# Merging two key blocks of a sliding-window attention before the exponentials, by a minimum, instead of behind them, by a sum

## The chip, the cores and the metric

One core of a Trainium2 chip runs the whole program. The metric is the time of one execution on the device, in microseconds (us); lower is better. The number to be predicted is the median after the change; the median before it is 2237.75 us.

## The reference, cut to what matters

Input `x` is 4 batches of 1024 rows of 1024 numbers, in fp32. Each row is normalised (`xn`). Then two branches are computed and joined as `x + s * g`:

- `s` is attention with 16 query heads, 4 key/value heads and a head size of 64. A query row `i` sees key `j` if `i - 511 <= j <= i`, or if `j < 4` (the sinks) and `j <= i`.
- `g` is the silu of a layer norm over `xn + gate * broadcast`: the gate is a sigmoid of a 1024x1024 product for every row, and the broadcast comes from a recurrent FFN on the last row of each batch (four steps, 1024 to 4096 and back).

The part that the change touches is this:

```python
att = jnp.einsum('bkgqd,bkjd->bkgqj', q, k) * scale
att = jnp.where(mask[None, None, None, :, :], att, -jnp.inf)
att = jax.nn.softmax(att, axis=-1)
y = jnp.einsum('bkgqj,bkjd->bkgqd', att, v)
```

## The kernel before, in words

The program has two stages. The first (`attend`) makes the projections, the attention and the FFN; it writes the attention's output `Y` and the split rows `XS` to HBM. The second (`finish`) makes the gate product and the output product for 32 tiles of 128 rows, and joins the branches. In the trace the first stage ends near 1515 us. Operands of the large products are split into a high and a low part (`x_hi`, `x_lo` and so on), and three products are summed.

**Units.** The attention of a batch is 32 units, numbered 0 to 31: 4 groups of 4 heads by 8 query blocks of 128 rows. Unit `s` has group `s // 8` and query block `qb = s % 8`. A unit's keys are the blocks in reach of the window, at most 5 of 128, each padded to 132 columns, with 4 sink columns behind them (`width_of`). With `qb` of 5, 6 or 7 (units 5 to 7, 13 to 15, 21 to 23, 29 to 31 of each batch, 48 in all) the farthest of the 5 blocks is in reach only above the diagonal, and the query's own block only on and below it. The two triangles fill one block of 128 columns. Such units are called merged (`is_merged`, L124).

**A unit's work.** TensorE makes the scores of heads 0 and 1 into `s_ps` (`scores`, L1033), later those of heads 2 and 3. VectorE adds the mask, turns the sign and scales, writes 660 columns to `probs` and takes the minimum of each row as `neg_max` (`mask_scores`, L1334, one custom operation and a short readout of the accumulator). ScalarE takes `exp(-1 * probs + neg_max)` over the same 660 columns and sums each row into `row_sum` (`exponentials`, L808). VectorE takes the reciprocal of two sums (`invert`, L1351), in merged units adds the farthest block's 128 columns onto the own block's (`merge`, L1357), and divides columns 132 to 660 (`divide`, L1363). One triangle of each block is masked, so that the sum holds one number of either. TensorE then transposes the blocks of the four heads into `t_ps` (`turn_probs`, L1071), ScalarE copies them to `pt` (`take_turned`, L798), POOL separates the merged block's two triangles again by two selects (`split_merged`, L700), and TensorE multiplies with `v` (`values`, L1094). POOL packs the 4 sink columns (`pack_sinks`, L712) behind the last division; they are transposed too, and VectorE's product `take_sinks` (L1389) spreads them into `pt_sink`, which the last matmul of `values` needs (L1131).

**The order of the work.** Each engine has one queue, written out by hand in its own `step(b, s)`. In the step of unit `u` the engines also finish unit `u - 1`:

- TensorE (L1167): scores of heads 0, 1; first two transposes of `u - 1` (they wait for all four divisions, `normed`); projections or FFN tiles; in some units the transpose of a row block of the next batch or of a weight (`turn_later`); scores of heads 2, 3 (they wait for both masks, `masked`); other transposes; projections; values of `u - 1`.
- ScalarE (L818): first copies of `u - 1`; exponentials of heads 0, 1; copies of the high parts of a turned block (`turned_high`, L796); copies; exponential 2; copy; exponential 3; others.
- VectorE (L1438): output copy of `u - 2` (`take_y`, L1387); masks of heads 0, 1; the FFN's sums (`add_sums`, L1423; `add_rows`, L1268); the low parts of a turned block (`turned_low`, L1332); masks of heads 2, 3; in units 21 to 28 the statistics of the next batch's rows (L87, L91); the first pair's reciprocal, sums and divisions; the product of the sinks of `u - 1`; the second pair's; in the same units the normalising of the next rows (L106). In units 26 to 31 of the last batch the split of gate weights stands last (L1499).

```python
def divide_pair(b, s, pair):
    invert(b, s, pair)
    for head in range(2 * pair, 2 * pair + 2):
        if is_merged(unit_of(s)[1]):
            merge(b, s, head)
    for head in range(2 * pair, 2 * pair + 2):
        divide(b, s, head)
```

Blocks are turned (`turned_in`) in units 22 to 29 of the first three batches, and weights in units 2, 4, 6, 10, 12, 18 and 20 of the first.

Of the kernel before, what the change touches and what calls it, by code (L numbers as in the profile page):

```python
# [21 lines left out]
ACT = mybir.ActivationFunctionType  # L22
ALU = mybir.AluOpType
AX = mybir.AxisListType

P = 128
# [8 lines left out]
WB = WINDOW // P  # L35
PADDED = P + 4
# [8 lines left out]
GROUP = HEADS // KV  # L45
UNITS = KV * TB
# [62 lines left out]
def unit_of(s):  # L109


    return s // TB, s % TB
# [11 lines left out]
def is_merged(qb):  # L124


    return qb > WB
# [42 lines left out]
def packed_before(u):  # L170

    return (TB - WB - 1) * (u // TB) + max(0, u % TB - WB - 1)
# [12 lines left out]
def attend(nc, shared, y_stored, WT, Y, BC, XS, x, gate_w, Wq, Wk, Wv, in_gamma, in_beta, agg_w, agg_b, pn_gamma, pn_beta, d1_w, d1_b, d2_w, d2_b,  # L185
           bc_w, bc_b):

    with ExitStack() as ctx:
        def sb(name, shape, dt=F32):
            return ctx.enter_context(nc.sbuf_tensor(name, shape, dt))  # L190
# [4 lines left out]
        def sem(name):  # L195
            return ctx.enter_context(nc.semaphore(name))
# [16 lines left out]
        probs = sb("probs", [P, 2 * GROUP, WIDTH])  # L213
# [71 lines left out]
        scores_ready, masked, exp_done = sem("scores_ready"), sem("masked"), sem("exp_done")  # L285
# [3 lines left out]
        merged, pt_split = sem("merged"), sem("pt_split")  # L289
# [137 lines left out]
        def width_of(qb):  # L427

            return blocks_of(qb) * PADDED - (0 if has_sink(qb) else SINK)
# [38 lines left out]
        with nc.Block() as block:  # L468
# [287 lines left out]
            def _(act):  # L756
# [51 lines left out]
                def exponentials(b, s, head):  # L808
                    _, qb = unit_of(s)
                    u = UNITS * b + s  # L810
                    width = width_of(qb)
                    slot = GROUP * (u % 2) + head
                    act.wait_ge(masked, GROUP * u + head + 1)
                    act.activation(probs[:, slot, 0:width], probs[:, slot, 0:width], ACT.Exp,  # L814
                                   bias=neg_max[:, slot:slot + 1], scale=-1.0,
                                   accum_out=row_sum[:, slot:slot + 1]).then_inc(exp_done, 1)

# [426 lines left out]
            def _(dve):  # L1244
# [89 lines left out]
                def mask_scores(b, s, head):  # L1334
# [6 lines left out]
                    if u == 0 and head == 0:  # L1341
# [6 lines left out]
                                             scale=-SCALE, scalar=-NEG, op0=ALU.add, op1=ALU.min,  # L1348
                                             accum_out=neg_max[:, slot:slot + 1]).then_inc(masked, 1)

                def invert(b, s, pair):  # L1351
                    u = UNITS * b + s
                    part = slice(GROUP * (u % 2) + 2 * pair, GROUP * (u % 2) + 2 * pair + 2)
                    dve.wait_ge(exp_done, GROUP * u + 2 * pair + 2)
                    dve.reciprocal(inv_sum[:, part], row_sum[:, part]).then_inc(inv_ready, 1)

                def merge(b, s, head):  # L1357

                    slot = GROUP * (UNITS * b + s) % (2 * GROUP) + head
                    own = probs[:, slot, WB * PADDED:WB * PADDED + P]  # L1360
                    dve.tensor_tensor(own, own, probs[:, slot, 0:P], ALU.add).then_inc(merged, 1)  # L1361

                def divide(b, s, head):  # L1363
                    _, qb = unit_of(s)
                    u = UNITS * b + s
                    slot = GROUP * (u % 2) + head
                    part = slice(PADDED if is_merged(qb) else 0, width_of(qb))
                    if head % 2 == 0:
                        dve.wait_ge(inv_ready, 2 * u + head // 2 + 1)
                    if is_merged(qb):  # L1370
                        dve.wait_ge(merged, GROUP * packed_before(u) + head + 1)
                    dve.tensor_scalar(probs[:, slot, part], probs[:, slot, part], inv_sum[:, slot:slot + 1], None,  # L1372
                                      ALU.mult).then_inc(normed, 1)

                def divide_pair(b, s, pair):
                    invert(b, s, pair)
                    for head in range(2 * pair, 2 * pair + 2):
                        if is_merged(unit_of(s)[1]):
                            merge(b, s, head)
                    for head in range(2 * pair, 2 * pair + 2):  # L1380
                        divide(b, s, head)

# [46 lines left out]
                def think(b):  # L1429
                    n = Q_LNS + LNS * b + TB  # L1430
                    dve.wait_ge(thought_ready, 2 + 2 * b)
                    ln_statistics(dve, ln, n, thought, B, st[0], mv[0])
# [5 lines left out]
                def step(b, s):  # L1438
                    u = UNITS * b + s
# [8 lines left out]
                        take_y(u - 2)  # L1448
                    mask_scores(b, s, 0)
                    mask_scores(b, s, 1)  # L1450
                    if b and s == 0:
                        if b == 1:
                            dve.wait_ge(bias_loaded, 32)
                        add_rows(b, thought, thought)
                        think(b)
# [18 lines left out]
                    if turned_in(b, s):  # L1474
                        for half in range(2):
                            turned_low(u, turned_in(b, s), half)
                    mask_scores(b, s, 2)
                    mask_scores(b, s, 3)
                    if ahead is not None:
                        stats(b + 1, ahead)  # L1480
                    divide_pair(b, s, 0)
                    take_place(1)
                    if u and has_sink((u - 1) % TB):
# [410 lines left out]
```

## Time and profile before

| what | value |
|---|---|
| times of three runs | 2233.90, 2237.75, 2241.33 us |
| median | 2237.75 us |
| the profiled execution: its time | 2241.33 us |
| its span in the trace | 2239.6 us |
| busy: PE, PEld (its weight loads), DVE, ACT, POOL | 2158.8, 1605.7, 1467.3, 840.9, 239.3 us |
| instructions of DVE, of ACT | 3265, 1793 |
| HBM traffic over the span | 163 GB/s |

PE is TensorE, DVE is VectorE, ACT is ScalarE, POOL is GpSimd, SP is the queue that issues most DMAs. Matmuls are pipelined, so that a busy PE can still be slower than its peak. A row of the trace can stand for several instructions in sequence (x2, x8). A bracket at the end of a row gives the idle time of that engine before it, and what ended it; "issue" is time in which it waited for nothing that the profile shows. Times within the trace count from the span's start.

### The profile page before, as it was taken

Reading aid. Unit: us, or ns where it says so; the run is one execution under the profiler, and the core shown is the slowest. Engines: PE = TensorE matmul, PEld = TensorE weight load, DVE = VectorE, ACT = ScalarE, POOL = GpSimd, SP = SyncE. Lnnn points to the kernel's source line nnn. Section 1 sums busy time; section 2 is a strip of 40 time slices with the busy share of each in tenths; the row PEclk is TensorE's granted clock in tenths of the full one; section 3 lists DMA queues with packets and bytes.
Section 4 is the critical chain, followed back from the end, with each engine's and each line's share of the span. In section 5 each row is a group of like instructions: output and inputs, shape, how many; then the busy total and the mean of one; then the engine's idle time right before and its main releaser. Section 6 shows DMA issues by size and latency. Waiting matters only on the chain. (4 is left out here: it accounts for less than half of the span.)

```text
span 2239.6 us, 35984 instructions
## 1 busy us (share of the span) xinstructions
PE 2158.8 (96%) x13433; PEld 1605.7 (72%) x13433; DVE 1467.3 (66%) x3265; ACT 840.9 (38%) x1793; POOL 239.3 (11%) x510
## 2 busy tenths in 40 slices
PE   7999999999999999999999999988999999999998
PEld 6666666766666676666676666657888888888886
DVE  6465677665667657567665566585676676767767
ACT  2254554444554435455343445462111111111111
POOL 2100111010002011011101000010101010010100
PEclk9999999999999999999999999999999999999999
DMA  7486459533447734545853354545333334243331
GB/s 255 137 275 216 129 186 298 167 134 120 152 159 251 245 104 149 179 137 193 283 173 119 122 185 165 201 165 184 141 109 144 122 122 143 101 150 99 144 132 56
DMA packets 174383, 366.57 MB, mean 164 GB/s; under 512 B 13320, under 2 KB 111880, under 8 KB 159904
## 3 DMA queue, kind: packets, MB, share of 16 engines
q1 hardware_dynamic: 168240, 348.30, 46.6%
q0 software_dynamic: 5568, 14.79, 1.9%
q8 instruction: 90, 1.47, 0.3%
q10 hardware_dynamic: 432, 1.57, 0.2%
q14 instruction: 53, 0.43, 0.1%
HBM read 284.79 MB, written 79.72 MB: 163 GB/s over the span
## 5 line engine op out<-in xcount | busy, mean ns | idle before, releaser
L805 ACT ACTIVATE pt<-t_ps 128x512 f32<-128x512 f32 x432 | 237.4, 595 | 475.4 <-PE t_ps L1090 474.9
L1022 PE MATMUL j_ps<-x_hi,w 128*128 128x512 f32 x1232 | 411.4, 404 | 0.0
L814 ACT ACTIVATE probs<-probs,neg_max 128x660 f32<-128x660 f32 (+5 forms) x512 | 356.8, 703 | 45.3 <-DVE neg_max L1344 45.0
L1344 DVE CUSTOM_DVE_ANT_0 probs<-s_ps,mask 128x660 f32<-128x660 f32 (+5 forms) x512 | 322.2, 667 | 68.4 <-PE s_ps L1057 66.6
L1747 PE MATMUL out_ps<-wo,w 128*128 128x512 f32 x1536 | 353.4, 389 | 2.6 <-DVE w L1804 2.6
L1747 PEld LDWEIGHTS out_ps<-wo,w 128*128 128x128 f32 x1536 | 288.3, 188 | 62.7 <-issue 3.0
L1747 PE MATMUL gate_ps<-x_hi,w 128*128 128x512 f32 x1024 | 281.5, 391 | 4.8 <-PEq L468 4.8
L1022 PEld LDWEIGHTS j_ps<-x_hi,w 128*128 128x128 f32 x1232 | 231.0, 190 | 54.4 <-issue 6.6
L1090 PE MATMUL t_ps<-ident,probs 128*128 128x128 f32 x1728 | 240.6, 280 | 24.4 <-DVE x_lo L1332 12.2
L1057 PE MATMUL s_ps<-k_hi,q 64*128 64x330 f32 (+5 forms) x1664 | 251.5, 330 | 8.8 <-DVE q L1316 5.6
L1057 PEld LDWEIGHTS s_ps<-k_hi,q 64*128 64x128 f32 x1664 | 160.0, 185 | 118.8 <-issue 61.6
L1022 PE MATMUL j_ps<-x_lo,w 128*128 128x512 f32 x616 | 244.2, 396 | 0.0
L1125 PE MATMUL o_ps<-pt,v 128*64 128x256 f32 x1920 | 236.5, 387 | 1.6 <-DVE small_rows L1276 1.4
L1090 PEld LDWEIGHTS t_ps<-ident,probs 128*128 128x128 f32 x1728 | 186.0, 141 | 68.0 <-issue 46.4
L1747 PEld LDWEIGHTS gate_ps<-x_hi,w 128*128 128x128 f32 x1024 | 192.9, 189 | 44.9 <-issue 5.0
L1372 DVE TENSOR_SCALAR probs<-probs,inv_sum 128x528 f32<-128x528 f32 (+5 forms) x512 | 207.1, 447 | 5.9 <-DVE probs L1361 0.3
L1125 PEld LDWEIGHTS o_ps<-pt,v 128*64 128x64 f32 x1920 | 127.1, 137 | 93.7 <-issue 42.1
L1734 ACT ACTIVATE b_res<-b_a 128x1024 f32<-128x1024 f32 x32 | 33.9, 1060 | 424.4 <-DVE b_a L1834 424.4
L1747 PE MATMUL gate_ps<-x_lo,w 128*128 128x512 f32 x512 | 158.5, 391 | 0.0
L907 PE MATMUL o_ps<-fw,cols 128*32 128x512 f32 x1088 | 141.9, 605 | 3.3 <-DVE y L1387 1.5
L1057 PE MATMUL s_ps<-k_lo,q 64*128 64x330 f32 (+5 forms) x832 | 135.5, 302 | 0.0
L1022 PEld LDWEIGHTS j_ps<-x_lo,w 128*128 128x128 f32 x616 | 117.1, 190 | 23.5
(182 smaller groups left out, 2317.5 us busy)
## 6 DMA issues: line engine op xcount, KB each, us to landing
fw<-in_L_ffn_d_w_dram SPq DMA_DIRECT2D x128, 1024.0 KB, 5.3
w<-WT SPq DMA_DIRECT2D x36, 1024.0 KB, 5.7
w<-XS SPq DMA_DIRECT2D x64, 512.0 KB, 6.4
XS<-x_hi SPq DMA_DIRECT2D x32, 512.0 KB, 6.9
XS<-x_lo SPq DMA_DIRECT2D x32, 512.0 KB, 8.0
Y<-y SPq DMA_DIRECT2D x256, 64.0 KB, 2.1
b_x<-in_L_attn_x_dram SPq DMA_DIRECT2D x32, 512.0 KB, 4.1
b_y<-Y SPq DMA_DIRECT2D x32, 512.0 KB, 6.5
```

The costliest lines, as they stand in the source:

```text
L805: act.activation(pt[:, m % PT_SLOTS, :, :], bank[:, :].rearrange("p (h q) -> p h q", q=P), ACT.Copy).then_inc(pt_ready, 1)
L814: act.activation(probs[:, slot, 0:width], probs[:, slot, 0:width], ACT.Exp, bias=neg_max[:, slot:slot + 1], scale=-1.0, accum_out=row_sum[ ...
L907: last = pe.matmul(f_ps[COLS * j:COLS * j + COLS, :], cols[:, B * first[j]:B * first[j] + COLS], fw[n % 2][:, bass.ts(j, BANK)], start=sta ...
L1022: last = pe.matmul(bank_of((kind, b, n)), w[:, slot, wp * C + c * P:wp * C + c * P + P], xs[:, c, bass.ts(ch, BANK)], start=i == 0, stop=i ...
L1057: last = pe.matmul(s_ps[head][:, BANK * part:BANK * part + width], qs[h, pair, bass.ts(qb, P)], k[h, g // 2, :, :].rearrange("p t c -> p ( ...
L1090: last = pe.transpose(t_ps[(turns_before(u) + i) % 2][:, bass.ts(head, P)], probs[:, GROUP * (u % 2) + head, PADDED * block:PADDED * block ...
L1125: last = pe.matmul(o_ps[HS * half:HS * half + HS, 0:2 * P], v[:, m * (1 + b % 2), qb - n + 1 + i, half, :], pt[:, (blocks_before(u) + i) % ...
L1344: dve.tensor_tensor_reduce(out=probs[:, slot, 0:width].rearrange("p (a n) -> p a n", a=parts), in0=s_ps[head % 2][:, :].rearrange("p (a n) ...
L1372: dve.tensor_scalar(probs[:, slot, part], probs[:, slot, part], inv_sum[:, slot:slot + 1], None, ALU.mult).then_inc(normed, 1)
L1734: act.activation(res[:, :], a[:, :], ACT.Sigmoid).then_inc(sig2_ready, 1)
L1747: last = pe.matmul(out_[:, bass.ts(half, BANK)], lhs[:, c, :], rhs(c, half), start=(c == 0 and lhs is hi and rhs is w_hi), stop=(c == KB - ...
```

## The change

In merged units the two blocks are merged before the exponential instead of after the reciprocal. At that point `probs` holds the sign-turned scores, in which a masked position is a huge positive number; the smaller of two numbers is the one that isn't masked. VectorE now takes this minimum of 128x128 once for each head, directly behind the masks of heads 0 and 1, and behind each of the masks of heads 2 and 3. Each minimum waits for its own head's mask. ScalarE's exponential waits for the minimum and takes columns 132 to 660, 528 instead of 660. The additions go. Units that aren't merged are unchanged.

```diff
--- before.py
+++ after.py
@@ -810,8 +810,12 @@
                     u = UNITS * b + s
                     width = width_of(qb)
                     slot = GROUP * (u % 2) + head
-                    act.wait_ge(masked, GROUP * u + head + 1)
-                    act.activation(probs[:, slot, 0:width], probs[:, slot, 0:width], ACT.Exp,
+                    part = slice(PADDED if is_merged(qb) else 0, width)
+                    if is_merged(qb):
+                        act.wait_ge(merged, GROUP * packed_before(u) + head + 1)
+                    else:
+                        act.wait_ge(masked, GROUP * u + head + 1)
+                    act.activation(probs[:, slot, part], probs[:, slot, part], ACT.Exp,
                                    bias=neg_max[:, slot:slot + 1], scale=-1.0,
                                    accum_out=row_sum[:, slot:slot + 1]).then_inc(exp_done, 1)
 
@@ -1348,17 +1352,21 @@
                                              scale=-SCALE, scalar=-NEG, op0=ALU.add, op1=ALU.min,
                                              accum_out=neg_max[:, slot:slot + 1]).then_inc(masked, 1)
 
+                def merge(b, s, head):
+
+                    u = UNITS * b + s
+                    if not is_merged(unit_of(s)[1]):
+                        return
+                    slot = GROUP * (u % 2) + head
+                    own = probs[:, slot, WB * PADDED:WB * PADDED + P]
+                    dve.wait_ge(masked, GROUP * u + head + 1)
+                    dve.tensor_tensor(own, own, probs[:, slot, 0:P], ALU.min).then_inc(merged, 1)
+
                 def invert(b, s, pair):
                     u = UNITS * b + s
                     part = slice(GROUP * (u % 2) + 2 * pair, GROUP * (u % 2) + 2 * pair + 2)
                     dve.wait_ge(exp_done, GROUP * u + 2 * pair + 2)
                     dve.reciprocal(inv_sum[:, part], row_sum[:, part]).then_inc(inv_ready, 1)
-
-                def merge(b, s, head):
-
-                    slot = GROUP * (UNITS * b + s) % (2 * GROUP) + head
-                    own = probs[:, slot, WB * PADDED:WB * PADDED + P]
-                    dve.tensor_tensor(own, own, probs[:, slot, 0:P], ALU.add).then_inc(merged, 1)
 
                 def divide(b, s, head):
                     _, qb = unit_of(s)
@@ -1367,16 +1375,11 @@
                     part = slice(PADDED if is_merged(qb) else 0, width_of(qb))
                     if head % 2 == 0:
                         dve.wait_ge(inv_ready, 2 * u + head // 2 + 1)
-                    if is_merged(qb):
-                        dve.wait_ge(merged, GROUP * packed_before(u) + head + 1)
                     dve.tensor_scalar(probs[:, slot, part], probs[:, slot, part], inv_sum[:, slot:slot + 1], None,
                                       ALU.mult).then_inc(normed, 1)
 
                 def divide_pair(b, s, pair):
                     invert(b, s, pair)
-                    for head in range(2 * pair, 2 * pair + 2):
-                        if is_merged(unit_of(s)[1]):
-                            merge(b, s, head)
                     for head in range(2 * pair, 2 * pair + 2):
                         divide(b, s, head)
 
@@ -1448,6 +1451,8 @@
                         take_y(u - 2)
                     mask_scores(b, s, 0)
                     mask_scores(b, s, 1)
+                    merge(b, s, 0)
+                    merge(b, s, 1)
                     if b and s == 0:
                         if b == 1:
                             dve.wait_ge(bias_loaded, 32)
@@ -1475,7 +1480,9 @@
                         for half in range(2):
                             turned_low(u, turned_in(b, s), half)
                     mask_scores(b, s, 2)
+                    merge(b, s, 2)
                     mask_scores(b, s, 3)
+                    merge(b, s, 3)
                     if ahead is not None:
                         stats(b + 1, ahead)
                     divide_pair(b, s, 0)
```

## Rows read from the trace of the kernel before

**Rows 1.** The page, section 1: busy time of each engine.
```profile
PE 2158.8 (96%) x13433; PEld 1605.7 (72%) x13433; DVE 1467.3 (66%) x3265; ACT 840.9 (38%) x1793; POOL 239.3 (11%) x510
```

**Rows 2.** Busy time by stretch of the span: an attention stretch, then one late unit (23).
```profile
450.00:804.00 354.00, 344.25 (x2476) 242.19 (x2476) 228.76 (x649) 171.54 (x405) 41.38 (x90) 1.00 0.54 175
...
330.73:342.47 11.74, 9.45 (x80) 5.88 (x81) 10.51 (x28) 6.68 (x14) 3.54 (x7) 1.00 0.94 303
```

**Rows 3.** Who waited for whom: us in total, times, longest us.
```profile
PE t_ps L1090 <- DVE probs L1372: 5.9, 10, 0.9
...
PE o_ps L1131 <- DVE pt_sink L1396: 4.6, 6, 0.8
...
DVE inv_sum L1355 <- ACT probs L814: 38.7, 47, 2.8
```

**Rows 4.** Groups of instructions by shape: busy us, mean ns, idle before.
```profile
L1361 DVE TENSOR_TENSOR probs<-probs 128x128 f32<-128x128 f32 x192 | 45.4, 278 | 0.0
...
L814 ACT ACTIVATE probs<-probs,neg_max 128x660 f32<-128x660 f32 x192 | 160.9, 845 | 3.2 <-DVE neg_max L1344 3.0
...
L814 ACT ACTIVATE probs<-probs,neg_max 128x524 f32<-128x524 f32 x64 | 46.1, 726 | 3.9 <-DVE neg_max L1344 3.8
```

**Rows 5.** Timeline of an ordinary merged unit: start us, us, engine, operation.
```profile
603.00 0.84 DVE L1344 CUSTOM_DVE_ANT_0 probs<-s_ps,mask 128x660 f32<-128x660 f32 x1
...
603.78 0.85 ACT L814 ACTIVATE probs<-probs,neg_max 128x660 f32<-128x660 f32 x1
...
604.27 0.69 DVE L1423 TENSOR_TENSOR rows<-o_ps,rows 128x512 f32<-128x512 f32 x1 [0.42 <-PE o_ps L907]
...
605.35 0.85 DVE L1344 CUSTOM_DVE_ANT_0 probs<-s_ps,mask 128x660 f32<-128x660 f32 x1 [0.38 <-PE s_ps L1057]
...
606.96 0.47 DVE L1361 TENSOR_TENSOR probs<-probs 128x128 f32<-128x128 f32 x2
...
607.35 0.89 DVE L1372 TENSOR_SCALAR probs<-probs,inv_sum 128x528 f32<-128x528 f32 x2
...
608.27 0.42 DVE L1396 TENSOR_TENSOR pt_sink<-t_ps,own_pair 48x256 fp32r<-48x256 f32 x1
...
611.91 0.18 PEld L1131 LDWEIGHTS o_ps<-pt_sink,v_sink 48*128 48x128 f32 x1 [0.39 <-issue]
```

**Rows 6.** Timeline of a unit that isn't merged.
```profile
500.66 0.16 DVE L1355 RECIPROCAL inv_sum<-row_sum 128x2 f32<-128x2 f32 x1
...
500.85 1.03 DVE L1372 TENSOR_SCALAR probs<-probs,inv_sum 128x656 f32<-128x656 f32 x2
```

**Rows 7.** Timeline of units 22 and 23 of batch 0.
```profile
329.33 0.38 PE L1131 MATMUL o_ps<-pt_sink,v_sink 48*128 48x256 f32 x1 [0.76 <-DVE pt_sink L1396]
...
330.73 0.86 PEld L1090 LDWEIGHTS t_ps<-ident,probs 128*128 128x128 f32 x8 [0.37 <-DVE probs L1372]
...
332.41 0.84 DVE L1344 CUSTOM_DVE_ANT_0 probs<-s_ps,mask 128x660 f32<-128x660 f32 x1
...
332.53 0.85 ACT L814 ACTIVATE probs<-probs,neg_max 128x660 f32<-128x660 f32 x1
...
334.33 1.09 ACT L796 ACTIVATE x_hi<-t_ps 128x512 fp32r<-128x512 f32 x2
...
342.47 1.09 PE L1090 MATMUL t_ps<-ident,probs 128*128 128x128 f32 x8 [0.73 <-DVE probs L1372]
```

**Rows 8.** Timeline of the end of the last batch.
```profile
1430.35 0.18 PEld L1131 LDWEIGHTS o_ps<-pt_sink,v_sink 48*128 48x128 f32 x1 [0.39 <-DVE pt_sink L1396]
...
1503.82 1.40 DVE L1268 TENSOR_TENSOR small_rows<-o_ps,small_rows 4x512 f32<-4x512 f32 x2
...
1510.05 1.09 PE L1090 MATMUL t_ps<-ident,probs 128*128 128x128 f32 x8 [0.83 <-DVE probs L1372]
```

**Rows 9.** Timeline of POOL: a select, and a copy beside VectorE's L1499.
```profile
603.48 0.64 POOL L706 TENSOR_SCALAR_AFFINE_SELECT pt<-pt 128x512 f32<-128x512 f32 x1 [2.43 <-ACT pt L805]
...
1499.73 2.27 POOL L717 CAST sink_cols<-probs 128x32 fp32r<-128x32 f32 x1 [6.99 <-DVE probs L1372]
```

## The prediction

> **What bounds the kernel now.** I read the page first. TensorE has work in 2158.8 of 2239.6 us, VectorE in 1467.3, ScalarE in 840.9 [rows 1]. By stretches, the attention stage keeps TensorE at 344 of 354 us, its clock granted in full, with VectorE at 229 us [rows 2]. The change touches VectorE and ScalarE only, and only in units whose query block is 5, 6 or 7: 3 of 8 per key group, 12 per batch, 48 in all. So the question is where TensorE waits for one of them. The waits answer it [rows 3]: TensorE stood still for the divided probabilities 10 times, 5.9 us in all, and for the sinks' product 6 times, 4.6 us. VectorE waited for exponentials 47 times, 38.7 us, but that is a wait of an engine that has slack. Whatever becomes of it is gained only where TensorE waits behind it.
>
> The profiled execution took 2241.33 us, 1.7 more than its span and 3.6 above the median of 2237.75. I work out a difference in its trace and add it to the median. About 0.3% (6.7 us) is what a measurement of this kernel can tell from no change.
>
> **The parts and their prices.** (1) *Shorter exponentials.* 192 exponentials go from 660 to 528 columns. One of 660 takes 0.845 us, one of 524 takes 0.726 [rows 4], so 0.12 us goes from each: 23 us of ScalarE, which is no bound.
>
> (2) *Merges out of the divisions.* 192 additions of 128x128 take 0.278 us each [rows 4]. In a pair they overlap: two take 0.47, and the divisions begin 0.08 before their end, so 0.39 per pair [rows 5]. Without them the first division waits for the reciprocal. The unmerged units show that wait: a reciprocal of 0.16 at 500.66, the division at 500.85, 0.03 after its end instead of 0.08 before it [rows 6]. So 0.39 - 0.11 = 0.28 us goes from in front of each pair's divisions.
>
> (3) *Minima instead.* No row has a 128x128 minimum of two tiles. The nearest is the sum of the same tiles, 0.278, the same operands under another operator, so I take that. As bounds I keep half and double of it, 0.14 and 0.56. The minima of heads 0 and 1 stand behind both masks and add 0.39. Those of heads 2 and 3 each wait for the mask operation just in front: they start 0.03 after its end, last 0.28, and the next starts 0.08 before their end. Against the old overlap of 0.08 that is 0.31 each, 0.62 for two.
>
> Of that wait the Trainium skill says otherwise (VectorE: DVE Perf Modes, The DRAIN you can't avoid): a semaphore between two Vector instructions costs nothing, since the pipe empties anyway. By it the two minima would add 0.40 and each pair would lose 0.39, and the sum below would be some 1.8 us lower (0.44 in each of four units). The rows differ: 0.11 us lies between start with and without a wait [rows 5, 6].
>
> (4) *Ordinary merged units.* At 603.00 the mask of head 1 starts and ends at 603.84. VectorE then idles 0.42 until 604.27, does the FFN sum and idles 0.38 until 605.35 [rows 5]. The 0.39 of minima fit into the first gap. If that cover were gone they would cost 0.39 in each of 48 units, 19 us. The first exponential starts near 604.1, when the first minimum is there, instead of 603.78 and the two give 0.24 back, so ScalarE is free for its next copies at most 0.1 later. Then the masks of heads 2 and 3 with minima are 0.62 later, the first divisions 0.62 - 0.28 = 0.34, the sinks' product 0.34, the last divisions 0.62 - 0.56 = 0.06. The sinks' product is done at 608.69 and TensorE comes to it at 611.91 [rows 5], so 0.34 is hidden. Price: nothing.
>
> (5) *The units where VectorE is the bound.* In units 22 and 23 of the first three batches (numbered from 0), VectorE also takes the next batch's rows (statistics, low parts, normalising): 10.5 busy of 11.7 us [rows 2]. In unit 22 TensorE stands 0.76 us for the sinks' product [rows 7]: it comes 0.34 later. It next waits for probabilities (0.37 between weight loads), which swallows a part; how much is left doesn't matter, since the longer wait of unit 23 comes right behind. In unit 23 the mask of head 0 ends at 332.49 and the exponential starts at 332.53. Head 1's mask ends at 333.25. Now the first exponential needs the first minimum: 333.17 + 0.28, with 0.06 from before and 0.04 for the signal, 333.55. That is 1.02 later. Two exponentials give back 0.24. ScalarE's copy of the turned rows, which follows them without a gap at 334.33, is 0.78 later, and with it the low parts, both masks and all that VectorE has behind them [rows 7]. The last divisions add 0.06. TensorE waited 0.73 us for them at 342.47; it goes on 0.84 later, which holds what was left of unit 22's delay. Price 3 x 0.84 = **2.5 us**. Unit 6 of batch 0 and units 29 turn a block too, but without VectorE's other load: I take nothing, and at worst another 0.84 each.
>
> (6) *The end of batch 3.* In unit 31 VectorE goes from head 1's mask straight to the last FFN rows (1503.82), so nothing hides the 0.39, and TensorE waits for the divisions at 1510.05 [rows 8]: 0.39 + 0.06 = **0.45 us** later. Where the last divisions wait for ScalarE they come up to 0.24 + 0.28 = 0.52 earlier; TensorE isn't waiting there, and I count nothing.
>
> No DMA is added, moved or renamed. The queues of SP and POOL keep their order. POOL's wait for the last division moves by 0.06.
>
> Sum: 2.5 + 0.45 = +3.0 us, so 2237.75 + 3.0 = **2240.7 us**, no change that can be told.
>
> **Rivals.** *A, slower: the sinks' product ends the values everywhere.* Place: the sinks' product stands between the two pairs of divisions and moves 0.34 later in all 48 merged units. If TensorE stands there each time, 48 x 0.34 = 16.3 us, 2254. It decides from the point where the product has less than 0.34 us to spare. For it: TensorE already waited there in 6 units. Against: at 608.69 against 611.91 it has 3.2 us, and in unit 22 of batch 3 the gap before the values' last weight load (1430.35) is 0.39, as without a wait at 611.91, though the profile names the product there [rows 5, 8]: near the point, not past it. Chance 0.08.
>
> *B, faster: the chain through the exponentials carries the end.* The last divisions would come 0.24 + 0.28 = 0.52 us earlier where they wait for ScalarE. The 10 stops for probabilities, 5.9 us in all, would go: 2231.9. If TensorE stood there in all the 47 places of VectorE's wait it would be 24 us, 2213, but rows 3 have only 10. Against it: at the largest of them (unit 23, unit 31) VectorE is busy, not waiting. Chance 0.08.
>
> *C: the minima of heads 0 and 1 now run beside POOL's selects.* Before, the sums never did. The select at 603.48 lasts 0.64 [rows 9] and a second follows it; the minima stand at 603.76 to 604.24. A POOL copy of 32 columns took 2.27 us beside VectorE operations with two SBUF operands [rows 9], so these two do share something, and there POOL was the one held. If POOL is held here too, its selects end up to 0.47 later, and TensorE needs them only in the second half of the values, which end near 612. If VectorE is held, which no row shows, the minima wait up to 0.36, or 1.06 behind both selects. That is hidden in ordinary units but delays unit 22's first exponential by up to 0.8 and unit 23's by 0.2: 3 x 1.0 = 3 us more, 2243.7. The Trainium skill (Advanced Engine Details and Errata, VectorE Performance Modes) has it that GpSimd and two-port Vector instructions share the second SBUF port and block each other. It names no loser. Chance of C: 0.11.
>
> **Chances.** Forecast 0.68, C 0.11, both within 0.3%: 0.79. A 0.08, and 0.05 for a later wait that I don't see: slower 0.13. B 0.08: faster. Range: the forecast gives -1 to +6 us (a minimum at 0.56 adds 0.56 or 0.84 us in each of the seven units of parts 5 and 6), the runs before spread over 2233.9 to 2241.3, and C adds 3. I give 2233 to 2248; A and the lower half of B lie outside.
>
> **What would show it.** Right: exponentials of 528 columns at 0.73 us; 192 minima at 0.28; TensorE's wait for unit 23's probabilities from 0.73 to about 1.5 us, three times; its wait for the sinks' product from 0.76 to about 1.1 in unit 22 and more in unit 23; ordinary merged units as long as before. Wrong: minima above 0.35 or POOL's selects above 0.64 (C); stops for the sinks' product in far more than 6 units (A); fewer stops for probabilities than 10 (B); a first exponential of unit 23 no later than before, which would take away my 2.5 us.

## The result: 0.2% slower, about 4.9 us

Over 22 runs each, the changed kernel took 2244.85 us (2241.31 to 2248.51), the kernel before 2241.01 (2232.76 to 2245.71). The ratio is 1.0022 with a 95% interval of 1.0014 to 1.0030: 4.9 us more, between 3.1 and 6.7. That is real and below the 0.3% that the prediction set as its bound. The time of 2240.7 was forecast from 2237.75, so +3.0, which lies just below this interval. Of the 4.2 us by which 2244.85 exceeds 2240.7, 3.3 are the kernel before itself: it took 2241.01 here, not 2237.75.

**The profile after.** The profiled execution took 2243.06 us, its span 2241.3. The page's busy times, which answer to [rows 1]:

```profile
PE 2155.3 (96%) x13433; PEld 1602.0 (71%) x13433; DVE 1490.3 (66%) x3265; ACT 824.8 (37%) x1793; POOL 243.2 (11%) x510
```

The groups by shape, which answer to [rows 4]: busy us, mean ns, idle before.

```profile
L1363 DVE TENSOR_TENSOR probs<-probs 128x128 f32<-128x128 f32 x192 | 57.9, 321 | 3.3
...
L818 ACT ACTIVATE probs<-probs,neg_max 128x528 f32<-128x528 f32 x192 | 140.4, 733 | 23.3 <-DVE probs L1363 23.2
...
L706 POOL TENSOR_SCALAR_AFFINE_SELECT pt<-pt 128x512 f32<-128x512 f32 x48 | 30.7, 639 | 117.3 <-ACT pt L805 117.3
...
L709 POOL TENSOR_SCALAR_AFFINE_SELECT pt<-pt 128x512 f32<-128x512 f32 x48 | 34.2, 713 | 3.3
```

ScalarE has its gift: 845 ns became 733, 192 times. VectorE didn't get the sum back for the same price: 278 ns became 321, and it is busy 23 us longer. The second of POOL's two selects, at 713 ns, was 637 before. The waits (us in total, times, longest) answer to [rows 3]. TensorE's for the sinks' product and for the low parts of turned rows grew (from 4.6 and 12.2); its wait for probabilities didn't:

```profile
PE t_ps L1094 <- DVE x_lo L1336: 14.8, 18, 1.3
...
PE o_ps L1135 <- DVE pt_sink L1399: 7.4, 7, 1.1
PE t_ps L1094 <- DVE probs L1378: 5.5, 11, 0.9
```

**Where the time went.** TensorE's order of work is the same in both kernels, so I measured from one output copy (`y<-o_ps`) to the next and compared the 127 steps. "The step of unit u" is the one in which VectorE masks and divides unit u.

| step of unit | before | after |
|---|---|---|
| 22, batches 0 to 2 | 13.30 | 13.45 |
| 23, batches 0 to 2 | 11.74 | 12.66 |
| 6, then 7, of batch 0 | 12.51, 13.34 | 12.83, 13.28 |
| 15, batch 3 | 10.33 | 10.64 |
| 22, batch 3 | 9.75 | 9.87 |
| 29, batch 3 | 10.97 | 10.46 |
| 31, batch 3 | 9.19 | 9.72 |

These sum to 3 x 1.07 + 0.26 + 0.31 + 0.12 - 0.51 + 0.53 = **+3.9 us**. The other merged units take the same time within 0.06 us, apart from two steps that differ without the change too. Unit 23 of batch 3 went from 9.43 to 9.12, but it is also 9.07 or 9.08 in three kernels with the old order there (experiments 2, 8 and 9). Unit 29 of batch 1 went from 16.00 to 16.37, but unit 28 in front of it from 14.29 to 14.00, and the kernel before, profiled again, has 14.35 and 16.06. In the last batch the steps of units 11, 28 and 30 are no measure: from profile to profile, whatever the kernel, they lie between 12.0 and 13.6, 9.2 and 10.6, 10.6 and 11.5. The timeline of units 22 and 23 of batch 0 shows how it comes about (against [rows 7]):

```profile
315.82 0.65 POOL L706 TENSOR_SCALAR_AFFINE_SELECT pt<-pt 128x512 f32<-128x512 f32 x1 [3.89 <-ACT pt L805]
...
316.10 0.71 DVE L1363 TENSOR_TENSOR probs<-probs 128x128 f32<-128x128 f32 x2
316.54 0.77 POOL L709 TENSOR_SCALAR_AFFINE_SELECT pt<-pt 128x512 f32<-128x512 f32 x1
...
328.49 0.64 POOL L709 TENSOR_SCALAR_AFFINE_SELECT pt<-pt 128x512 f32<-128x512 f32 x1
...
328.77 0.69 DVE L1363 TENSOR_TENSOR probs<-probs 128x128 f32<-128x128 f32 x2
...
329.30 0.74 ACT L818 ACTIVATE probs<-probs,neg_max 128x528 f32<-128x528 f32 x1 [1.11 <-DVE probs L1363]
...
330.75 1.06 ACT L796 ACTIVATE x_hi<-t_ps 128x512 fp32r<-128x512 f32 x2
...
332.57 0.83 DVE L1348 CUSTOM_DVE_ANT_0 probs<-s_ps,mask 128x660 f32<-128x660 f32 x1
...
332.80 1.06 PE L1094 MATMUL t_ps<-ident,probs 128*128 128x128 f32 x8 [1.31 <-DVE x_lo L1336]
...
333.45 0.29 DVE L1363 TENSOR_TENSOR probs<-probs 128x128 f32<-128x128 f32 x1
333.65 0.84 DVE L1348 CUSTOM_DVE_ANT_0 probs<-s_ps,mask 128x660 f32<-128x660 f32 x1
...
337.85 0.38 PE L1135 MATMUL o_ps<-pt_sink,v_sink 48*128 48x256 f32 x1 [1.14 <-DVE pt_sink L1399]
...
338.98 1.09 PE L1094 MATMUL t_ps<-ident,probs 128*128 128x128 f32 x8 [0.46 <-DVE probs L1378]
```

Read it from 328.77. The two minima take 0.69 where two sums took 0.47 [rows 5], since POOL's second select lies beside them. ScalarE has stood idle 1.11 us for the first one. Behind the two exponentials comes the copy of turned rows, and TensorE waits 1.31 us for the low parts made from it (0.55 before), then 1.14 for the sinks' product (0.76 before). It finds the last divisions a little nearer: 0.46 instead of 0.73. The two other waits in the kernel before:

```profile
336.40 1.07 PE L1090 MATMUL t_ps<-ident,probs 128*128 128x128 f32 x8 [0.55 <-DVE x_lo L1332]
...
341.07 0.38 PE L1131 MATMUL o_ps<-pt_sink,v_sink 48*128 48x256 f32 x1 [0.76 <-DVE pt_sink L1396]
```

The sum 0.76 + 0.38 - 0.27 is 0.87 of the step's 0.92. One minimum between two masks costs 1.08 from start to start instead of 0.76: 0.32.

**The minima and the selects.** The single instructions, as number and shortest, median and longest ns: the minima and the second select after, then the second select before.

```profile
L1363 DVE TENSOR_TENSOR probs<-probs x192: 276/291/510, 134.3 to 1507.5; 128x128 f32<-128x128 f32 x192
L709 POOL TENSOR_SCALAR_AFFINE_SELECT pt<-pt x48: 636/770/776, 145.9 to 1512.5; 128x512 f32<-128x512 f32 x48
...
L709 POOL TENSOR_SCALAR_AFFINE_SELECT pt<-pt x48: 636/637/640, 150.7 to 1512.2; 128x512 f32<-128x512 f32 x48
```

In 30 of the 48 units the pair of minima meets a select, and each time the one that started later is the one that lasts longer. A select that is already under way keeps its 0.64 us, and the first minimum takes 0.49 to 0.51; the second takes 0.28. In 27 units the second select starts beside the minima, and takes 0.77. In unit 22 above, the first minimum (316.10, 0.51) ends 0.14 behind the select that started at 315.82.

**Units 15 and 29 of batch 3.** In unit 15 the minima stand in front of an FFN result (`h_pre`) that TensorE waits for. Before, after, and with the doubled minima of experiment 4:

```profile
1345.78 0.42 PE L1057 MATMUL s_ps<-k_hi,q 64*128 64x330 f32 x2 [0.32 <-DVE h_pre L1406]
...
1346.82 0.42 PE L1061 MATMUL s_ps<-k_hi,q 64*128 64x330 f32 x2 [0.64 <-DVE h_pre L1409]
...
1348.48 0.42 PE L1061 MATMUL s_ps<-k_hi,q 64*128 64x330 f32 x2 [1.48 <-DVE h_pre L1415]
```

In unit 29 VectorE waits less for the last exponentials, and the output copy behind its last divisions, for which TensorE waits at the start of unit 30, comes sooner. Two rows before, two after:

```profile
1487.72 0.17 DVE L1355 RECIPROCAL inv_sum<-row_sum 128x2 f32<-128x2 f32 x1 [0.94 <-ACT probs L814]
...
1491.75 2.01 PE L907 MATMUL o_ps<-fw,cols 128*32 128x512 f32 x16 [1.52 <-DVE y L1387]
...
1487.77 0.17 DVE L1369 RECIPROCAL inv_sum<-row_sum 128x2 f32<-128x2 f32 x1 [0.34 <-ACT probs L818]
...
1491.54 1.92 PE L911 MATMUL o_ps<-fw,cols 128*32 128x512 f32 x16 [1.05 <-DVE y L1390]
```

Whether this gain of 0.5 lasts to the end isn't shown, since the step of unit 30 differs by more from profile to profile.

### The profile page after: what moved, and what is told of

Its sections match the earlier page's. It is cut to its first block and busy times, and to the rows that moved or that the text cites. A ratio compares the mean times of both kernels' runs of the same rounds, so it can differ in the third digit from the quotient of the medians.

```text
span 2241.3 us, 35888 instructions
## 1 busy us (share of the span) xinstructions
PE 2155.3 (96%) x13433; PEld 1602.0 (71%) x13433; DVE 1490.3 (66%) x3265; ACT 824.8 (37%) x1793; POOL 243.2 (11%) x510
## 5 line engine op out<-in xcount | busy, mean ns | idle before, releaser
L818 ACT ACTIVATE probs<-probs,neg_max 128x528 f32<-128x528 f32 (+5 forms) x512 | 336.3, 661 | 65.1 <-DVE neg_max L1348 41.7
```

The costliest lines, as they stand in the source:

```text
L818: act.activation(probs[:, slot, part], probs[:, slot, part], ACT.Exp, bias=neg_max[:, slot:slot + 1], scale=-1.0, accum_out=row_sum[:, slo ...
```

## Experiments

All are built from one of the two kernels. Each experiment is compared with runs of the kernel before taken beside it; experiments 5 to 8 are one run each, beside one run of the kernel before, on another chip than the other experiments. The steps below come from their profiles.

**1 and 2. Old order in the seven turned units; new order there alone.** The seven are units 22 and 23 of batches 0 to 2 and unit 6 of batch 0. The first keeps the change elsewhere:

```diff
+def ahead_of(u):
+    b, s = divmod(u, UNITS)
+    return is_merged(s % TB) and (not ((b < B - 1 and s in (22, 23)) or (b == 0 and s == 6)))
...
-                    if not is_merged(unit_of(s)[1]):
+                    if not ahead_of(u):
```

> The changed kernel, but units 22 and 23 of batches 0 to 2 and unit 6 of batch 0 keep the sum behind the exponentials. Theory T (the cost lies where a turned block's copy stands behind the late first exponential: 0.32 us in unit 6, 1.08 us per batch in units 22 and 23, 3.5 us in all): the steps of these units are again as long as before (11.74 us for unit 23), and the time is about 3.5 us below the changed kernel's, at 1.0000 to 1.0007 of the kernel before. Rival R (the cost is spread over all 48 merged units, whose minima run beside POOL's selects and last longer): only 7 of 48 parts go, the ratio stays near 1.0019.

The second is the same with the `not` ahead of the bracket left out.

> The mirror: the kernel before, with the minimum ahead in those seven units alone. T: plus 3.5 us, ratio to the kernel before 1.0015, unit 23's step 12.7 us instead of 11.74, all other merged steps as before. R: plus 0.7 us at most, ratio 1.0003.

Measured: the first 2241.34, ratio 1.0015 (0.9997 to 1.0032), the second 2244.67, ratio 1.0030 (1.0016 to 1.0044). The steps moved as a switch does: 11.74, 13.30 and 12.52 with the old order in those units, 12.66, 13.45 and 12.81 with the new. So these seven units carry 3.5 of the 3.9 us by steps. The times alone don't decide between theory and rival: the first interval holds what both expected (up to 1.0007, and 1.0019), and the second is 6.4 us above the kernel before where 3.5 were expected. The ratio of the first lies 0.0015 above 1 with little in its steps; the section on the clock takes that up.

**3. A minimum behind each mask for all four heads.**

```diff
-                    mask_scores(b, s, 1)
                     merge(b, s, 0)
+                    mask_scores(b, s, 1)
```

> The changed kernel with the order mask 0, minimum 0, mask 1, minimum 1. The first exponential then starts 0.35 us after its old place instead of 1.0, but head 1's mask ends 0.31 later, and TensorE's second scores wait for it. T: unit 23's step falls from 12.66 to about 12.2, units 22 and 23 give back 1 to 1.5 us in all; in ordinary units TensorE comes to that mask 0.29 after its end, so up to 0.05 in each is lost, 2 us: ratio to the kernel before 1.001 to 1.003. R (the VectorE time of the minima is what costs): each minimum behind its mask adds a wait of 0.11, so 0.2 in each of 48 units, 10 us more than the changed kernel, ratio 1.006.

Measured: 2247.9, ratio 1.0045 (1.0028 to 1.0063). Unit 23 gained (12.33 instead of 12.66), since the first exponential starts earlier, but most ordinary merged units lost 0.07 to 0.12 (up to 0.05 was expected), a loss that the changed kernel doesn't have. The ratio lies above the theory's 1.003 and below the rival's 1.006, and its interval reaches both. Units 15 and 31 of batch 3 lost 0.5 more than in the changed kernel (11.13 and 10.24). The gap behind head 1's mask covers a pair of minima there; in front of that mask nothing does.

**4. Twice the minima for heads 0 and 1.** Two more minima of 128x128, on constants, follow in each of the 48 units.

```diff
+                        for n in range(2):
+                            part = mask4[:, 2 * P * n:2 * P * n + P]
+                            dve.tensor_tensor(part, part, part, ALU.min)
```

> The changed kernel with two more 128x128 minima (of a constant tile with itself, which changes nothing) behind those of heads 0 and 1 in all 48 merged units, about 0.4 us of VectorE each. T: they lie in VectorE's idle time, 0.3 us before the FFN sum and 0.4 before head 2's mask in ordinary units, and 1.25 before the low parts in unit 23, so only what exceeds it shows: plus 0 to 4 us on the changed kernel. R: 0.4 in each of 48 units, plus 19 us, ratio to the kernel before about 1.011.

Measured: 2248.63, ratio 1.0050 (1.0030 to 1.0070). Ordinary merged units kept their length even with this load. A theory that the loss is spread over all 48 has to fall: it is in the units where VectorE is late already. Of the 3.8 us above the changed kernel's time, 2.4 are the step of unit 15 of batch 3 (13.04 instead of 10.64), where TensorE's wait for the FFN result grew to 1.48 us.

**5. POOL's selects wait for the minima.**

```diff
+                    if is_merged((u + 1) % TB):
+                        pool.wait_ge(merged, GROUP * packed_before(u + 1) + 2)
```

> The changed kernel, with POOL's selects waiting for the minima of heads 0 and 1 where the next unit is merged too, so that they no longer run beside them. If the selects hold up VectorE: minima of units 22, 23 and their like go from 0.69 to 0.71 us per pair back to 0.47, the mean of 192 from 0.32 to about 0.28, the first exponential of units 22 and 23 starts about 0.2 earlier, and the two steps give back 0.2 to 0.4 us per batch of the 1.08. Rival (the minimum is a slower operation than the sum): the pair stays at 0.7.

Measured, one run: 2242.57 beside 2238.43. The groups by shape of this kernel:

```profile
L1365 DVE TENSOR_TENSOR probs<-probs 128x128 f32<-128x128 f32 x192 | 51.5, 289 | 3.3
...
L711 POOL TENSOR_SCALAR_AFFINE_SELECT pt<-pt 128x512 f32<-128x512 f32 x48 | 30.6, 638 | 3.3
```

Its timeline ahead of unit 23's exponentials:

```profile
327.19 0.49 DVE L1365 TENSOR_TENSOR probs<-probs 128x128 f32<-128x128 f32 x2
...
327.84 0.65 POOL L708 TENSOR_SCALAR_AFFINE_SELECT pt<-pt 128x512 f32<-128x512 f32 x1 [2.06 <-DVE probs L1365]
```

Kept apart, both have their own duration again: 0.49 instead of 0.69, 638 ns instead of 713. Unit 23's step fell to 12.45 (-0.21), unit 22's to 13.41 (-0.04), unit 6's to 12.60 (-0.22), that of unit 15 of batch 3 to 10.44 (-0.20). This is what the contention costs.

**6. Exponentials at their old width.** The exponentials take all 660 columns again, so that the farthest block counts twice in the row sums.

```diff
-                    part = slice(PADDED if is_merged(qb) else 0, width)
+                    part = slice(0, width)
```

> The changed kernel with exponentials over all 660 columns (the sum of a row then counts the farthest block twice over, so that the output is another). T: the 0.12 us per exponential matter only where TensorE waits behind ScalarE: unit 23's step 12.66 to about 12.9, unit 6's 12.83 to 13.07, three batches: plus 1 us, and the gains of batch 3 in steps 29 and 30 (0.5 each) go half away. Rival (shorter exponentials gained nothing): no step moves.

Measured, one run: 2240.93 beside 2238.43; the steps of units 23, 22 and 6 grew to 12.89, 13.67 and 13.05, 0.22 or 0.23 more each: two exponentials of 0.12. Unit 29 of batch 3 lost half of its gain (10.71 instead of 10.46). The shorter exponentials do pay, but only where ScalarE is waited for. The run's total is lower than the changed kernel's although these steps are longer: its mean clock is 0.995, and unit 11 of batch 3 is 0.8 shorter in it. A single run doesn't tell 2 us.

**7. The minima of heads 2 and 3 in a pair.** Both follow head 3's mask, so that neither minimum waits for the mask right in front of it: head 2's mask is done, and head 2's minimum stands between head 3's mask and its minimum.

```diff
-                    merge(b, s, 2)
                     mask_scores(b, s, 3)
+                    merge(b, s, 2)
                     merge(b, s, 3)
```

> The changed kernel with the minima of heads 2 and 3 both behind mask 3, so that no minimum waits for the mask right in front except the last. My price of the wait (0.11 us each): steps of units 22 and 23 are 0.1 to 0.25 shorter together per batch. By the rule that such a wait is free: no step moves.

Measured, one run: 2247.3 beside 2238.43, with steps of 13.20 and 12.43 in units 22 and 23 (-0.25 and -0.23). The pair takes 0.49 and overlaps the work behind it, where single ones cost 0.32 each, so the wait just behind a mask is not free: 0.12 for each of the two. The time itself says nothing here, at a mean clock of 0.990, the lowest of the single runs. Unit 29 lost 0.31 of its gain, probably since head 2's exponential starts later.

**8. The kernel before with a load in unit 23.** One minimum of 128x640 on constants in front of head 2's mask.

```diff
+                    if b < B - 1 and s == 23:
+                        dve.tensor_tensor(mask4[:, 0:5 * P], mask4[:, 0:5 * P], mask4[:, 0:5 * P], ALU.min)
```

> The kernel before, with one 128x640 minimum of a constant tile with itself (0.8 us of VectorE, changes nothing) before head 2's mask in unit 23 of batches 0 to 2, so that TensorE waits longer there as in the changed kernel, with no merge moved. Theory K (TensorE's longer wait in unit 23 is what brings the 3.4 us at granted clock 0.5 right behind it, seen behind 1 of 3 such units in the kernel before and behind 2 or 3 of 3 with the new order): unit 23's step 12.5 us and the slow stretch behind 2 or 3 of 3. Rival (it comes by chance or by the new order itself): behind 0 or 1 of 3.

The load and TensorE's wait in this kernel's timeline:

```profile
333.08 0.81 DVE L1478 TENSOR_TENSOR mask<-mask 128x640 f32<-128x640 f32 x1
...
338.71 0.39 PE L1131 MATMUL o_ps<-pt_sink,v_sink 48*128 48x256 f32 x1 [1.49 <-DVE pt_sink L1396]
```

Measured, one run: 2243.91 beside 2238.43. Some 0.73 us more on VectorE's row (the next mask starts that much later) made TensorE wait 0.73 longer (1.49 for 0.76) and the step 0.74 longer (12.48 for 11.74). Unit 23 has no slack on VectorE in front of head 2's mask: what goes in comes out in the step, one for one. The sign of theory K came too: all three places behind unit 23 show a lowered clock.

**9. The sum behind the exponentials, made by POOL.** If unit 23 has no slack, what leaves VectorE should come back as well. From the kernel before, with the old sum, in units 22 and 23 of batches 0 to 2 and unit 31 of batch 3:

```diff
+                def merge_pair(u, pair):
+                    if not on_pool(u):
+                        return
+                    for head in range(2 * pair, 2 * pair + 2):
+                        slot = GROUP * (u % 2) + head
+                        own = probs[:, slot, WB * PADDED:WB * PADDED + P]
+                        pool.wait_ge(exp_done, GROUP * u + head + 1)
+                        pool.tensor_tensor(own, own, probs[:, slot, 0:P], ALU.add).then_inc(merged, 1)
...
-                        if is_merged(unit_of(s)[1]):
+                        if is_merged(unit_of(s)[1]) and not on_pool(UNITS * b + s):
                             merge(b, s, head)
```

> The kernel before with the sum behind the exponentials kept, but made by POOL instead of VectorE in the seven units that VectorE bounds: 22 and 23 of batches 0 to 2 and 31 of the last batch (28 sums of 128x128). Theory (in these units VectorE's own row is the bound, so what leaves it is gained, and the end of the values moves with the sum, which is not the bound there): 0.28 us per pair is saved where the pair stood between VectorE's mask and its next work, so the steps behind units 22 and 23 become together about 0.6 to 1.1 us shorter in each of three batches and unit 31 about 0.5, 2.5 to 4 us in all: ratio to before about 0.9985. Rival (the values' end, or POOL itself, becomes the bound): POOL's sum of two sources lasts longer than VectorE's 278 ns and stands behind its selects, the last divide and the sinks' product go on waiting for the exponentials, and nothing is gained: ratio 1.000, or a step up to 0.5 us longer in each.

POOL's group of this kernel:

```profile
L725 POOL TENSOR_TENSOR probs<-probs 128x128 f32<-128x128 f32 x28 | 12.5, 454 | 6.2 <-ACT probs L833 5.9
```

Its timeline in unit 23 of batch 0:

```profile
332.18 0.86 POOL L725 TENSOR_TENSOR probs<-probs 128x128 f32<-128x128 f32 x2
332.21 0.42 DVE L1415 TENSOR_TENSOR pt_sink<-t_ps,own_pair 48x256 fp32r<-48x256 f32 x1
...
332.69 0.38 PE L1150 MATMUL o_ps<-pt_sink,v_sink 48*128 48x256 f32 x1 [0.49 <-DVE pt_sink L1415]
332.87 0.96 DVE L1391 TENSOR_SCALAR probs<-probs,inv_sum 128x528 f32<-128x528 f32 x2
```

Measured: **2231.1 us (8 runs), ratio 0.9955 (0.9940 to 0.9971)**, faster than both kernels. POOL needs 454 ns for what VectorE does in 278, but it has the time. The wait for the sinks' product is 0.49 instead of 0.76, and the steps are 12.83 and 11.25 in units 22 and 23 and 8.82 in unit 31, so 3 x 0.96 + 0.37 = 3.2 us less, as expected. The ratio is worth 10 us, where 0.9985 was expected. The rest isn't in these steps.

**10. The change only where it might gain**, in units 21 to 23, 29 and 30 of batch 3 (`return is_merged(s % TB) and b == B - 1 and s in (21, 22, 23, 29, 30)`).

> The change only in five merged units of the last batch (21, 22, 23, 29, 30), old order everywhere else. Theory (the shorter exponentials gain only where the profile of after showed a shorter step that no clock drop explains, behind unit 29): that step is about 0.5 us shorter than in the kernel before (10.97), the steps behind 21 to 23 within 0.15 of before where both have full clock, and the time is the kernel before's less 0.5: ratio about 0.9998, not to be told from 1. Rival (the shorter steps of the last batch in the profile of after were all gains of the change): 0.3 for unit 22's, 0.5 for unit 27 or 28's and 0.5 for unit 29's, 1.0 to 1.3 us in all: ratio 0.9995.

Measured: 2237.75 (12 runs) beside 2240.2, ratio 0.9989 (0.9976 to 1.0002), not to be told from 1. Unit 29's step is 10.45, the 0.5 expected; unit 23's is 9.11, but the ninth experiment has 9.08 there with the old order. What the step of unit 29 gains can't be seen in the time.

**11 and 12. Both kernels once more.**

> The changed kernel once more, letter for letter, for its granted clock: theory 1 (the longer waits of TensorE behind units 22 and 23 of batches 0 to 2 bring a stretch of half clock more often than before's) has at least two of the three stretches behind those units show a clock below 1; theory 2 (the places are chance) has none or one. Ratio to before 1.0015 to 1.003 by the steps alone, as before.

> The kernel before once more, letter for letter, for its granted clock: theory 1 (as for the changed kernel) has at most one of the three stretches behind units 22 and 23 show a clock below 1; theory 2 (chance) has two or three as often as the changed kernel. The steps behind units 22 and 23 are 13.30 and 11.74 us in both.

Measured: the changed kernel 2245.0 (12 runs), ratio 1.0021 (1.0009 to 1.0034); the kernel before 2241.17 in one run. The same steps came again (13.45 and 12.66; 13.30 and 11.74). Behind unit 23, one of three places had a lowered clock in the changed kernel and two of three in the kernel before: theory 1 has no support in these two profiles.

**What the clock adds.** In a few places of each execution the granted clock falls to half, 1.2 GHz, for a few microseconds. The same step of the kernel before, behind unit 23, with and without it (start and end, length, busy times, then the clock's mean):

```profile
343.00:356.70 13.70, 12.51 (x88) 8.87 (x85) 7.76 (x26) 5.38 (x15) 3.09 (x7) 1.00 0.71 212
...
1067.40:1082.40 15.00, 14.01 (x87) 9.53 (x86) 7.80 (x25) 5.49 (x15) 3.09 (x7) 0.89 0.59 186
```

That is 1.3 us for one such place in this cut, and 1.4 to 1.6 in the step of unit 24, which takes 15.0 to 15.2 instead of 13.6 where it has one. A profile shows between one and five of them from the first output copy to the last. They don't lie anywhere: 46 of the 50 in the 14 profiles are behind unit 23 of a batch, around unit 1 of the next, or near unit 28 of the last batch. Which of these places have one differs from run to run. Each run records its mean clock. Over the 142 runs of the compared sets, fitted with one slope and one level for each set, 0.001 of mean clock goes with 1.67 us (standard error 0.10). Levels at a clock of 0.993, with errors of 0.4 to 0.8:

| kernel | runs | mean clock | time at 0.993 | against before |
|---|---|---|---|---|
| before (two sets) | 25, 25 | 0.9932, 0.9920 | 2238.5, 2238.7 | |
| after (two sets) | 22, 12 | 0.9916, 0.9915 | 2242.5, 2242.6 | +3.9 |
| 1, old order in turned units | 12 | 0.9916 | 2239.0 | +0.4 |
| 2, new order there alone | 12 | 0.9913 | 2241.8 | +3.1 |
| 3, alternating | 8 | 0.9919 | 2245.3 | +6.7 |
| 4, doubled | 6 | 0.9917 | 2246.6 | +8.0 |
| 10, new in batch 3 alone | 12 | 0.9931 | 2238.2 | -0.4 |
| 9, sum on POOL | 8 | 0.9948 | 2234.1 | -4.5 |

At equal clock the times agree with the steps: +3.9 against the table's +3.9; -4.5 against -3.2 by the steps named, with an error of 0.8; near nothing for the first. What is left of each ratio goes with the mean clock. The ninth kernel's profile has none of these stretches behind units 22 and 23, and one from the first output copy to the last; this part takes 1403.5 us in it, and 1410.5 and 1414.0 in the two profiles of the kernel before, which have three and four.

Why it has fewer stays open. The waits of TensorE ahead of those places are shorter in it, and the counts behind unit 23 lean that way: none of 3 in the ninth kernel, 5 of 12 with the waits of the kernel before (that kernel twice, experiments 1 and 10), 18 of 27 with longer ones (the changed kernel twice, experiments 2 to 8). But the changed kernel alone has 3 of 6 like the kernel before, and the first experiment has a low mean clock with the old waits. That longer waits bring more such stretches isn't shown.

## Why the prediction held, and where not

- **Parts (1) and (2)** stood. 733 ns was forecast as 726 to 730; the exponentials' gain is 0.22 for two where it is waited for (experiment 6).
- **Part (3)**: one minimum alone takes 0.29, and one behind a waiting mask 0.32 (0.31 forecast). The term that was mis-sized is the pair of heads 0 and 1: 0.39 was taken, for a pair that lasts 0.47, but beside the selects it lasts 0.69 to 0.71. Experiment 7 bears out the wait: pairing the last two minima gives back 0.25 and 0.23 for two waits. By the Trainium skill (VectorE: DVE Perf Modes, The DRAIN you can't avoid), a semaphore between two Vector instructions costs nothing; the 0.11 that the rows gave in the prediction holds here, and the measurement decides.
- **Part (4)**, nothing in ordinary merged units, held even with twice the minima (experiment 4). Behind the order of experiment 3 it would not have held.
- **Part (5)** found the right place and the right path (minimum, exponential, copy of turned rows, low parts). Its size was 0.84 per batch and measured 1.07. The contention of experiment 5, 0.21 + 0.04, is that difference: without it 0.82 is left. The first exponential of unit 23 starts 2.39 us behind the output copy instead of 1.21, so 1.18 later where 1.02 was forecast. Which wait shows the delay was wrong: I named the last divisions with 1.5 us; it was the low parts (1.31) and the sinks' product (1.14), and the divisions' wait fell to 0.46. The path sets the sum, not the wait in which it surfaces. "Unit 6 of batch 0 and units 29: I take nothing" failed twice: unit 6 costs 0.32, and unit 29 of batch 3 gains 0.51, since there TensorE waits for an output copy that stands behind the last exponentials. I didn't look at unit 15 of batch 3 at all; the minima stand there in front of an FFN result that TensorE waits for (0.32 before, 0.64 after), and it costs 0.31.
- **Part (6)**: 0.45 forecast, 0.53 measured.
- **Rivals.** A fell: stops for the sinks' product went from 6 to 7. B fell as a total, though unit 29 is B in one unit. C was true as a mechanism, with either engine held by the one that started first (0.22 us on the pair, 0.13 on the second select where it meets the minima), at 3 x 0.25 = 0.75 us in units 22 and 23 instead of 3, and 0.2 each in unit 6 and unit 15 of batch 3. The Trainium skill (Advanced Engine Details and Errata, VectorE Performance Modes) has GpSimd and two-port Vector instructions block each other on the shared port. The trace agrees that they get in each other's way (0.28 us became 0.50, 0.64 became 0.77). The page doesn't say whether a minimum of two tiles counts as a two-port instruction, and these rows don't tell a full stop from a slower pace.
- The forecast +3.0 against +3.9 by the steps is thus contention (0.75), unit 6 and unit 15 (0.6) and small ones, less unit 29 (0.5). That the sum came so near is partly luck: a loss and a gain of about 0.5, neither of them foreseen, cancel. The 4.9 of the ratio holds about 1 us more, within its interval, of which the steps show nothing; the clock's stretches were not in my range's working.

## What to carry to other kernels

Find the units in which the engine that you load has no idle time between two waits of the bottleneck, and price only those; a gift to an idle engine and a load in a covered gap are both worth nothing. If such a unit is found, the better change is to take work off that engine in it: POOL made the same sum 1.6 times slower, and the time fell by 0.45%, of which 4.5 us (0.2%) stand at equal clock. Judge differences of 0.2% by step lengths in the trace or at equal mean clock, since a few half-clock stretches are as large.

## What was not expected of the hardware

- VectorE's 128x128 minimum of two SBUF tiles and POOL's 128x512 select lengthen each other, and it is the later one that pays: the first minimum of a pair takes 0.50 us instead of 0.28 beside a select under way, a select that starts beside the minima 0.77 instead of 0.64.
- A minimum that waits for the mask right in front of it costs 0.12 us more than one in a pair behind both masks (experiment 7).
- POOL's own 128x128 sum of two sources took 454 ns, VectorE's 278.
- TensorE's granted clock falls to 1.2 GHz for a few microseconds at one to five of the same few places of the attention stage, in which of them differs from run to run, each worth 1.3 to 1.6 us.
